# Another order of the attention's extras on four engines

## The chip, the cores and the metric

The kernel runs on one core of one Trainium2 chip. The metric is the device time of one execution in microseconds (us): smaller is better. A core has TensorE (PE, with its weight loads shown as PEld), VectorE (DVE), ScalarE (ACT), GpSimd (POOL) and SyncE (SP, whose queue issues most DMAs). Each takes its own list of instructions in order; they meet in semaphores.

## The reference

One transformer layer with adaptive layer norm, on x of 8 x 512 x 128: an attention with 16 heads of 8 columns, causal, with a layer norm on its output, and then a mixture of 8 experts of which each token uses 2.

```python
mod = (_silu(c) @ wmod).reshape(8, 6, 1, -1)          # sa, ca, ga, sb, cb, gb
h = _layernorm(x) * (1 + ca) + sa
q, k, v = h @ Wq.T, h @ Wk.T * scale, h @ Wv.T
attn = softmax(where(causal, q_heads @ k_heads.T, -inf))
x = x + ga * ((_layernorm(attn @ v_heads) * gamma + beta) @ Wo.T)
h = _layernorm(x) * (1 + cb) + sb
x = x + gb * sum(top-2 experts e: weight_e * (silu(h @ gate_e.T) * (h @ up_e.T)) @ down_e.T)
```

## The kernel before

The attention goes through 8 batches `b` of 512 tokens, each in 4 steps `g` = 0 to 3 of 4 heads; the text calls them the first to the fourth step. Behind its 32 steps comes the loop over 71 tiles of 128 tokens for the experts, which the change doesn't touch.

Each engine has a function `step(b, g)`, a hand-written list of calls for each `g`. TensorE's list is built round two rows of units that take turns. `nat(b, g, k)`, k = 0 to 10 (lines 536 and 538), computes scores of the step two ahead with the tokens on partitions, in bank `psN[k % 4]`, for VectorE's `maxima(k)` (line 1415), which takes each row's maximum. `scores(b, g, u)`, u = 0 to 9 (lines 551 and 553), computes this step's scores transposed, less the maxima, in bank `psT[u % 2]`, for ScalarE's `exps(u)` (line 1098). A `nat` waits for the `maxima` of four units before, a `scores` for the `exps` of two units before. A unit of 512 columns takes 0.22 us on TensorE.

Between these units stand the extras, whose places the change moves:

- `values(b, g, c)`, c = 0 to 3 (line 570): probabilities times v for one chunk of key tokens, 512, 384, 128 and 256 columns wide, each of 4 heads with a weight tile 32 columns wide. They fill bank `psO`; ScalarE's `keep_values` (line 1105) empties it.
- `turn_values` (line 578) transposes that output into `psM`; VectorE's `normalise` (lines 1421, 1425) divides it.
- `turn_max` (line 584) transposes the maxima, split by VectorE into `max_high` and `max_low` (lines 1387, 1392), with a weight tile 32 columns wide; ScalarE's `keep_max` copies them to `mrow` (line 1092), and SP's `max_rows` (line 434) sends them into row 0 and 1 of the next step's stack, for which the next step's `scores` 0 waits.
- `turn_x`, `project_q`, `project_k`, `project_v` (lines 591 to 606): the next batches' x, q, k and v. ScalarE's `x_norm`, `shift_in` and `high`, VectorE's `residue` and `middle` and POOL's `low` split q and k in three bf16 parts; SP sends them out (`q_out`, `k_out`, lines 411, 415) and the stacks for a later step in (`stacks_in`, lines 385, 427, 428).
- `turn_attn` (line 613), `project_o` (line 619) with ScalarE's `o_norm` and `keep_attn` (line 1110) and VectorE's `o_stats`, `mean_var` and `gate_out` (line 1434): the output projection of the batch before.
- `turn_h`, `experts`, `rank` (lines 632 to 656) with ScalarE's `keep_h` (line 1121), `keep_z` and `exp_bids` and VectorE's `route` of 27 short links: the router of the batch two before.

All extras but `values` share the one bank `psM`. `take` on TensorE makes each of them wait until the bank's last user has been read:

```python
def take(free=None):
    if bank[0] is not None:
        pe.wait_ge(*bank[0])
    bank[0] = free
```

SP's queue sets a second order. In the second step (`g == 1`) it first waits for the landing of all six parts of q and k of the next batch, then issues seven DMAs for a stack, and only then `max_rows`:

```python
if g == 1:
    hold("sp", sp, qk_out, 96 * (b + 2))
hold("sp", sp, t_full, UNITS * (4 * b + g))
stacks_in(*step_at(b, g, 3))
max_rows(*step_at(b, g, 1))
```

`k_out` in turn waits for VectorE's `middle` of k (line 1397) and POOL's `low` (line 2035) in the first step. In the last batch's third step VectorE also builds the experts' tile table (`table`, lines 1763 to 1775).

## Time and profile before

| | |
|---|---|
| median of 3 runs | 612.96 us (611.4 to 614.01) |
| the profiled execution | 611.13 us, span 609.4 us |
| TensorE busy | 552.1 us (91%), 5257 matmuls |
| VectorE busy | 470.1 us (77%) |
| ScalarE busy | 404.2 us (66%) |
| GpSimd busy | 244.4 us (40%) |
| chain that ended last | 75% of the span on TensorE, 7% VectorE, 5% issue, 4% DMA |
| granted TensorE clock, mean | 0.966 |

The attention's steps run from about 42 to 358 us of the span, 39.5 to 40.0 us a batch from the third to the sixth; the experts fill the rest. Matmuls overlap in the trace: a row's length is longer than its share of TensorE's time, so the distance from start to start is what a unit costs. A weight load (PEld) with idle time ahead of it doesn't tell by itself whether TensorE waited or was still streaming.

### The profile page before, as it was taken

The page shows a single profiled execution, that of the slowest core. Times are in us where ns is not written, and L with a number is a line of the kernel's source. Part 1 is how long each engine was busy: PE and PEld are TensorE (multiplying, and loading weights), DVE is VectorE, ACT ScalarE, POOL GpSimd, SP SyncE. Part 2 cuts the span into 40 slices and gives each one's busy share as a digit, 9 for nine tenths or more (in the row PEclk, how much of TensorE's full clock was granted, in tenths as well). Part 3 has the DMA queues.
Part 4 walks back from the last instruction along what each step waited for, and adds up shares of the span by engine and source line. Part 5 has one row for each costly group of instructions (what it writes and reads, how often), then busy time and mean ns, then how long its engine had stood idle before and what let it go on. Part 6 is the DMA issues. An engine that isn't in the chain of part 4 may idle for free.

```text
span 609.4 us, 16545 instructions
## 1 busy us (share of the span) xinstructions
PE 552.1 (91%) x5257; PEld 416.9 (68%) x5258; DVE 470.1 (77%) x1593; ACT 404.2 (66%) x715; POOL 244.4 (40%) x328
## 2 busy tenths in 40 slices
PE   5787999999999999999999989999889999999920
PEld 2464555666566566575666549998779999999920
DVE  5899778889899899898998757875846666667635
ACT  4424788888878888788778876765445656565511
POOL 5401301041453643535535345666553333333326
PEclk9597999999999999999999999999999999999975
DMA  4441576732242332333331011122422211111147
GB/s 124 133 139 53 152 209 178 206 98 81 72 123 83 89 105 81 114 88 94 109 98 55 16 42 42 41 58 65 109 67 54 54 44 51 46 46 51 36 176 250
DMA packets 61511, 56.82 MB, mean 93 GB/s; under 512 B 11156, under 2 KB 55572, under 8 KB 61444
## 3 DMA queue, kind: packets, MB, share of 16 engines
q1 hardware_dynamic: 56548, 44.88, 26.6%
q0 software_dynamic: 4320, 8.99, 4.7%
q10 hardware_dynamic: 576, 2.10, 0.9%
q8 instruction: 37, 0.61, 0.4%
q14 instruction: 30, 0.25, 0.1%
HBM read 36.92 MB, written 18.45 MB: 91 GB/s over the span
## 4 chain that ended last, share of the span: by engine, by line
PE 75%; DVE 7%; issue 5%; DMA 4%; ACT 3%; POOL 2%; SPq 1%; another core or an unknown queue 1%; POOLq 0%; ACTq 0%; DVEq 0%
PE psN L970 16%; PE psO L570 13%; PE psO L981 8%; PE psT L551 8%; PE psN L536 7%; PE psT L553 5%; PE psN L538 5%; PE psM L578 2%; DMA probs<-expert_out 2%; DVE negm L1415 1%; PE psM L596 1%; PE psM L601 1%; PE psM L644 1%; PE psM L606 1%; PE psT L957 1%
## 5 line engine op out<-in xcount | busy, mean ns | idle before, releaser
L1415 DVE TENSOR_REDUCE negm<-psN 128x1 f32<-128x512 f32 (+3 forms) x352 | 210.9, 636 | 31.5 <-PE psN L538 27.2
L1098 ACT ACTIVATE probs<-psT 128x512 f32<-128x512 f32 x320 | 180.4, 595 | 40.4 <-PE psT L553 32.1
L970 PE MATMUL psN<-probs 128*128 128x128 f32 x1136 | 139.5, 275 | 0.7 <-issue 0.4
L970 PEld LDWEIGHTS psN<-probs 128*128 128x128 f32 x1136 | 132.6, 192 | 1.6 <-issue 1.5
L2177 POOL DMA_INDIRECT expert_out<-kst_all,dest x71 | 69.1, 973 | 108.2 <-DVE kst_all L1932 98.5
L536 PE MATMUL psN<-kst_all,qst_all 74*128 74x256 bf16 (+2 forms) x384 | 101.2, 281 | 6.2 <-DVE negm L1415 4.1
L551 PE MATMUL psT<-qst_all,kst_all 74*128 74x256 bf16 (+2 forms) x384 | 99.7, 277 | 1.6 <-DMA qst_all<-mrow 0.6
L570 PE MATMUL psO<-probs,vaug 128*32 128x512 f32 (+3 forms) x1024 | 93.7, 444 | 0.1
L538 PE MATMUL psN<-kst_all,qst_all 117*128 117x128 bf16 x512 | 91.7, 222 | 0.0
L1292 ACT ACTIVATE probs<-gu_w 128x1024 f32 x70 | 74.0, 1057 | 24.8 <-PE psN L970 20.0
L1908 DVE TENSOR_TENSOR probs<-probs,psN 128x512 f32<-128x512 f32 x71 | 48.7, 686 | 53.4 <-PE psN L970 22.7
L553 PE MATMUL psT<-qst_all,kst_all 117*128 117x128 bf16 x512 | 85.6, 221 | 0.0
L981 PE MATMUL psO<-down_w,probs 128*128 x568 | 76.4, 278 | 9.3 <-DVE kst_all L1932 8.9
L1300 ACT ACTIVATE probs<-psN 128x512 f32<-128x512 f32 x71 | 42.3, 595 | 61.8 <-PE psN L970 49.5
L981 PEld LDWEIGHTS psO<-down_w,probs 128*128 128x128 f32 x568 | 69.0, 192 | 11.5 <-issue 11.5
L2069 POOL DMA_INDIRECT dispatched<-rows,slots x56 | 56.6, 1010 | 49.4 <-ACT probs L1098 39.9
L536 PEld LDWEIGHTS psN<-kst_all,qst_all 74*128 74x128 bf16 x384 | 38.9, 102 | 41.0 <-DVE negm L1415 22.5
L551 PEld LDWEIGHTS psT<-qst_all,kst_all 74*128 74x128 bf16 x384 | 37.4, 99 | 37.7 <-ACT probs L1098 21.2
L538 PEld LDWEIGHTS psN<-kst_all,qst_all 117*128 117x128 bf16 x512 | 46.8, 100 | 12.9 <-issue 6.3
L553 PEld LDWEIGHTS psT<-qst_all,kst_all 117*128 117x128 bf16 x512 | 50.8, 99 | 1.9
L570 PEld LDWEIGHTS psO<-probs,vaug 128*32 128x32 f32 x1024 | 21.1, 108 | 21.6 <-issue 13.2
L1932 DVE TENSOR_SCALAR kst_all<-psO,dsc 128x128 f32<-128x128 f32 x71 | 24.8, 349 | 13.2 <-PE psO L981 12.6
(242 smaller groups left out, 739.5 us busy)
## 6 DMA issues: line engine op xcount, KB each, us to landing
qst_all<-q_parts_dram SPq DMA_DIRECT2D x96, 96.0 KB
kst_all<-k_parts_dram SPq DMA_DIRECT2D x96, 96.0 KB
kst_all<-dispatched SPq DMA_DIRECT2D x71, 66.0 KB
q_parts_dram<-qparts SPq DMA_DIRECT2D x24, 128.0 KB
k_parts_dram<-kparts SPq DMA_DIRECT2D x24, 128.0 KB
xall<-in_x SPq DMA_DIRECT2D x8, 256.0 KB, 3.4
gu_w<-in_gateT SPq DMA_DIRECT2D x4, 512.0 KB, 5.1
gu_w<-in_upT SPq DMA_DIRECT2D x4, 512.0 KB, 4.9
```

The source lines that it names most:

```text
L536: pe.matmul(psN[:, k % NBANKS, col:col + w - P], qst[g][0:KALL, j, tb * P:(tb + 1) * P], kst[g][0:KALL, j, 0:w - P], start=True, stop=True)
L538: mm = pe.matmul(psN[:, k % NBANKS, col + w - P:col + w], qst[g][0:KMASK, j, tb * P:(tb + 1) * P], kst[g][0:KMASK, j, w - P:w], start=True ...
L551: pe.matmul(psT[:, u % TBANKS, col + P:col + S - P * blk], kst[g][0:KALL, j, blk * P:(blk + 1) * P], qst[g][0:KALL, j, (blk + 1) * P:S], s ...
L553: mm = pe.matmul(psT[:, u % TBANKS, col:col + P], kst[g][0:KMASK, j, blk * P:(blk + 1) * P], qst[g][0:KMASK, j, blk * P:(blk + 1) * P], st ...
L570: mm = pe.matmul(psO[32 * j:32 * j + 32, blk * P:S], vaug[:, blk, g * J + j, :], probs[:, g % 2, o:o + w], start=(c == 0), stop=(c == TB - 1))
L970: mm = pe.matmul(bank[par][:, c * P:(c + 1) * P], ew[par][:, half, c * P:(c + 1) * P], xgT[par], start=True, stop=True)
L981: mm = pe.matmul(psY, hh[par][:, c * P:(c + 1) * P], down_w[:, bass.ds(e, 1), c, :], start=(c == 0), stop=(c == FC - 1))
L1098: nc.scalar.activation(probs[:, g % 2, 512 * u:512 * (u + 1)], psT[:, u % TBANKS, :], ACT.Exp, scale=SOFTMAX_SCALE).then_inc(exp_done, 1)
L1292: nc.scalar.activation(ew[par][:].rearrange("p k f -> p (k f)"), gu_w[:, bass.ds(e, 1)].rearrange("p o k f -> p (o k f)"), ACT.Copy).then_ ...
L1415: nc.vector.tensor_reduce(dst, src, axis=AX.X, op=ALU.max, negate=True).then_inc(nat_done, 1)
L2069: gp.indirect_dma_start(xd[:, :], bass.IndirectOffsetOnAxis(ap=slots_of(b)[:, k, n:n + 1], axis=0), rows_of(b)[:, n, :], None).then_inc(di ...
L2177: gp.indirect_dma_start(yd[:, :], bass.IndirectOffsetOnAxis(ap=dest[u][:, 0:1], axis=0), ysb[u], None).then_inc(y_out[u], 16)
```

## The change

No instruction is added or taken away. In `step` of TensorE, ScalarE and VectorE, calls change places; POOL's and SP's lists stay. TensorE's new lists, with the units as n0 to n10 (`nat`) and s0 to s9 (`scores`) and the `values` as V0 to V3:

```text
step 1 before: n0 s0 n1 s1 V1 n2 s2 turn_values n3 s3 n4 V2 turn_max s4 n5 s5 project_k n6 s6 n7 s7 V3 n8 s8 turn_h n9 s9 n10 experts
step 1 after:  n0 s0 n1 s1 V1 n2 s2 turn_values n3 s3 V2 n4 turn_max s4 n5 s5 project_k n6 s6 V3 n7 s7 n8 turn_h s8 n9 s9 n10 experts
step 2 before: n0 s0 n1 s1 n2 turn_values V0 s2 n3 s3 V1 n4 s4 V2 turn_max n5 s5 n6 V3 s6 n7 s7 project_v n8 s8 n9 s9 V0 V1 n10
step 2 after:  n0 s0 n1 s1 turn_values n2 V0 s2 n3 s3 V1 turn_max n4 s4 n5 V2 s5 V3 n6 s6 n7 s7 project_v n8 s8 V0 n9 s9 V1 n10
step 3 before: n0 s0 rank n1 s1 n2 s2 turn_attn n3 s3 n4 V2 s4 turn_values n5 s5 n6 s6 turn_max n7 s7 n8 V3 s8 n9 s9 project_o n10
step 3 after:  rank n0 s0 n1 s1 n2 V2 s2 turn_attn n3 s3 n4 s4 turn_values n5 s5 n6 s6 turn_max n7 s7 n8 V3 s8 n9 s9 n10 project_o
step 4 before: n0 s0 n1 s1 V0 n2 s2 turn_values n3 s3 n4 s4 V1 n5 s5 n6 s6 n7 turn_max V2 s7 n8 V3 s8 turn_x n9 s9 n10 V0 project_q
step 4 after:  n0 s0 n1 s1 V0 n2 s2 n3 s3 n4 turn_values s4 n5 s5 V1 n6 s6 V2 n7 turn_max s7 n8 V3 s8 n9 s9 turn_x V0 n10 project_q
```

The core of the diff, with the other engines:

```diff
@@ TensorE, first step
-                    if there(b, g, 2):
-                        nat(*step_at(b, g, 2), 4)
                     if there(b, g, -1):
                         values(*step_at(b, g, -1), 2)
+                    if there(b, g, 2):
+                        nat(*step_at(b, g, 2), 4)
                     if there(b, g, 1):
                         turn_max(*step_at(b, g, 1))
...
@@ TensorE, second step
                     scores(b, g, 8)
+                    values(b, g, 0)
                     if there(b, g, 2):
                         nat(*step_at(b, g, 2), 9)
                     scores(b, g, 9)
-                    values(b, g, 0)
+                    values(b, g, 1)
...
@@ ScalarE, first step
                         keep_h(b - 2)
+                    exps(b, g, 8)
                     if there(b, g, -1):
                         keep_values(*step_at(b, g, -1))
-                    exps(b, g, 8)
...
@@ ScalarE, second step: keep_max ahead of exps 4; third o_norm and exp_bids ahead of exps 9
@@ ScalarE, third step: keep_values ahead of exps 9
@@ ScalarE, fourth step: first x_norm ahead of exps 0, fourth ahead of exps 6
@@ VectorE, first step
-                    if there(b, g, 2):
-                        maxima(*step_at(b, g, 2), 0)
                     if there(b, g, 1):
                         max_high(*step_at(b, g, 1))
+                    if there(b, g, 2):
+                        maxima(*step_at(b, g, 2), 0)
...
                         residue(b + 1, k_hi, kparts, kres, k_r1, k_parts)
-                        middle(b + 1, kres, kparts, k_r1, k_mid)
...
                         maxima(*step_at(b, g, 2), 8)
+                    if has_batch(b + 1):
+                        middle(b + 1, kres, kparts, k_r1, k_mid)
+                    if there(b, g, 2):
                         maxima(*step_at(b, g, 2), 9)
...
@@ VectorE, second step: max_high ahead of maxima 0; mean_var behind maxima 4; single route links move by one maximum
@@ VectorE, third step
-                    if has_batch(b - 1):
-                        gate_out(b - 1)
                     if b == B - 1:
                         table(slice(0, N1), nfull, None)
                         V.nop().then_inc(tiles_ready, 1)
+                    if has_batch(b - 1):
+                        gate_out(b - 1)
...
@@ VectorE, third and fourth step: max_high behind maxima 0 and 1; normalise of the fourth behind maxima 4
```

## Rows read from the trace of the kernel before

**Rows 1.** Stretches: width, busy us of each engine (instructions), granted clock, DMA.
```profile
245.50:285.10 39.60, 39.58 (x419) 25.12 (x418) 35.60 (x108) 32.97 (x70) 18.54 (x26) 1.00 0.33 96
...
323.20:357.60 34.40, 33.17 (x346) 19.05 (x343) 27.77 (x97) 28.81 (x59) 14.22 (x20) 1.00 0.14 39
```

**Rows 2.** Waits of the weight loads, 126 to 323 us: total, times, longest.
```profile
PEld psN L536 <- DVE negm L1415: 11.6, 20, 0.8
PEld psT L551 <- ACT probs L1098: 10.3, 24, 0.8
```

**Rows 3.** Timeline around chunks 0 and 1 of values: start, length, [idle before <-releaser].
```profile
257.53 0.10 PEld L551 LDWEIGHTS psT<-qst_all,kst_all 74*128 74x128 bf16 x1 [0.84 <-ACT probs L1098]
...
258.15 0.22 PE L553 MATMUL psT<-qst_all,kst_all 117*128 117x128 bf16 x1
...
259.09 0.28 PE L536 MATMUL psN<-kst_all,qst_all 74*128 74x256 bf16 x1
...
274.81 0.22 PE L553 MATMUL psT<-qst_all,kst_all 117*128 117x128 bf16 x1
...
275.96 0.34 PE L536 MATMUL psN<-kst_all,qst_all 74*128 74x384 bf16 x1
```

**Rows 4.** Timeline, TensorE's weight loads behind three waits.
```profile
253.63 0.29 PEld L641 LDWEIGHTS psM<-confb,onesrow 1*128 1x128 f32 x2 [0.19 <-ACT h2T L1121]
...
267.29 0.10 PEld L551 LDWEIGHTS psT<-qst_all,kst_all 74*128 74x128 bf16 x1 [0.18 <-ACT probs L1098]
...
279.29 0.10 PEld L551 LDWEIGHTS psT<-qst_all,kst_all 74*128 74x128 bf16 x1 [0.21 <-ACT probs L1098]
```

**Rows 5.** Timeline of TensorE, third step: values 2 and turn_max apart.
```profile
268.53 0.22 PE L538 MATMUL psN<-kst_all,qst_all 117*128 117x128 bf16 x1
268.68 0.43 PE L570 MATMUL psO<-probs,vaug 128*32 128x128 f32 x8
269.04 0.28 PE L551 MATMUL psT<-qst_all,kst_all 74*128 74x256 bf16 x1
...
270.40 0.28 PE L553 MATMUL psT<-qst_all,kst_all 117*128 117x128 bf16 x2
...
270.76 0.28 PE L536 MATMUL psN<-kst_all,qst_all 74*128 74x256 bf16 x1
```

**Rows 6.** Timeline of TensorE around values 2 with turn_max, first and fourth step.
```profile
248.31 0.22 PE L538 MATMUL psN<-kst_all,qst_all 117*128 117x128 bf16 x1
...
248.85 0.28 PE L551 MATMUL psT<-qst_all,kst_all 74*128 74x256 bf16 x1
...
279.64 0.22 PE L538 MATMUL psN<-kst_all,qst_all 117*128 117x128 bf16 x1
...
280.17 0.28 PE L551 MATMUL psT<-qst_all,kst_all 74*128 74x256 bf16 x1
```

**Rows 7.** Timeline of TensorE around values 0 and 1, end of second step.
```profile
263.67 0.22 PE L553 MATMUL psT<-qst_all,kst_all 117*128 117x128 bf16 x1
...
265.46 0.40 PE L538 MATMUL psN<-kst_all,qst_all 117*128 117x128 bf16 x4
```

**Rows 8.** Timeline, third step: turn_attn, keep_attn, turn_values.
```profile
267.47 0.42 PEld L613 LDWEIGHTS psM<-identf,onn 128*128 128x128 f32 x4
...
268.22 0.77 ACT L1110 ACTIVATE lnT<-psM,bet,gam 128x512 f32<-128x512 f32 x1
...
269.22 0.42 PEld L578 LDWEIGHTS psM<-identf,oT 128*128 128x128 f32 x4
```

**Rows 9.** Timeline of VectorE, last batch's third step.
```profile
349.98 0.69 DVE L1434 TENSOR_TENSOR proj<-psM,modbc 128x512 f32<-128x512 f32 x1 [0.25 <-PE psM L619]
```

**Rows 10.** SP's queue in the second step; the chain around 232 us.
```profile
256.44 0.76 SPq L385 DMA_DIRECT2D qst_all<-zero_b  x1
...
261.49 1.21 SPq L434 DMA_DIRECT2D qst_all<-mrow  x2
...
231.71 2.93 DMA qst_all<-mrow
```

More of the change, by code:

```diff
@@ L703, in step @@
                     scores(b, g, 6)
+                    if there(b, g, -1):
+                        values(*step_at(b, g, -1), 3)
                     if b == B - 1:
@@ L744, in step @@
                         values(*step_at(b, g, -1), 1)
+                    if there(b, g, 1):
+                        turn_max(*step_at(b, g, 1))
                     if there(b, g, 2):
@@ L788, in step @@
                         nat(*step_at(b, g, 2), 2)
+                    if there(b, g, -1):
+                        values(*step_at(b, g, -1), 2)
                     scores(b, g, 2)
@@ L796, in step @@
                         nat(*step_at(b, g, 2), 4)
-                    if there(b, g, -1):
-                        values(*step_at(b, g, -1), 2)
                     scores(b, g, 4)
@@ L839, in step @@
                     scores(b, g, 2)
-                    if there(b, g, -2):
-                        turn_values(*step_at(b, g, -2))
                     if there(b, g, 2):
@@ L846, in step @@
                         nat(*step_at(b, g, 2), 4)
+                    if there(b, g, -2):
+                        turn_values(*step_at(b, g, -2))
                     scores(b, g, 4)
+                    if there(b, g, 2):
+                        nat(*step_at(b, g, 2), 5)
+                    scores(b, g, 5)
                     if there(b, g, -1):
@@ L850, in step @@
                     if there(b, g, 2):
-                        nat(*step_at(b, g, 2), 5)
-                    scores(b, g, 5)
-                    if there(b, g, 2):
                         nat(*step_at(b, g, 2), 6)
                     scores(b, g, 6)
+                    if there(b, g, -1):
+                        values(*step_at(b, g, -1), 2)
                     if there(b, g, 2):
@@ L859, in step @@
                         turn_max(*step_at(b, g, 1))
-                    if there(b, g, -1):
-                        values(*step_at(b, g, -1), 2)
                     scores(b, g, 7)
@@ L1208, in step @@
                     exps(b, g, 8)
+                    if there(b, g, -1):
+                        keep_values(*step_at(b, g, -1))
                     exps(b, g, 9)
@@ L1211, in step @@
                         keep_spread(LATER[4 * b + g], psM[:])
-                    if there(b, g, -1):
-                        keep_values(*step_at(b, g, -1))
                 elif g == 3:
+                    if has_batch(b + 2):
+                        x_norm(b + 2, (0,))
                     exps(b, g, 0)
@@ L1591, in step @@
                     if has_batch(b - 2):
+                        route(b - 2, 6)
                         route(b - 2, 7)
+                    if there(b, g, 2):
+                        maxima(*step_at(b, g, 2), 3)
                     if has_batch(b - 1):
@@ L1693, in step @@
                     if there(b, g, 2):
-                        maxima(*step_at(b, g, 2), 1)
                         maxima(*step_at(b, g, 2), 2)
-                        maxima(*step_at(b, g, 2), 3)
-                    if there(b, g, -2):
-                        normalise(*step_at(b, g, -2))
                     if there(b, g, 1):
@@ L1701, in step @@
                     if there(b, g, 2):
+                        maxima(*step_at(b, g, 2), 3)
                         maxima(*step_at(b, g, 2), 4)
+                    if there(b, g, -2):
+                        normalise(*step_at(b, g, -2))
                     if has_batch(b - 1):
```

103 lines of the change are left out of this document (47 added, 56 removed).

## The prediction

> **What bounds the kernel now.** I first looked at the stretches of the span [rows 1]. A batch of attention in steady state (the sixth of eight) takes 39.6 us, as do its neighbours; TensorE is busy in practically all of it, at the full granted clock; VectorE is busy 35.6 us of it and ScalarE 33. So in this part the order of TensorE's own queue sets the time, and another engine counts only where TensorE waits for it. In the last batch (323 to 357 us) TensorE has 1.2 us of idle time and ScalarE is the busier neighbour. Behind 357.6 us the experts run; the diff touches nothing there.
>
> Next the list of waits of the weight loads [rows 2]. It claims 11.6 us for VectorE's maxima and 10.3 us for ScalarE's exponentials between 126 and 323 us. Before I believe it I look at where these waits lie. The longest, 0.84 us, follow chunk 0 of `values`, and every other long one a chunk as well: from the last start ahead of it to the first behind it chunk 0 (512 columns) takes 1.15 us, chunk 1 (384) 0.94 [rows 3], the gap growing with the chunk whatever engine is named. That is four heads streaming side by side, hence work. Real waits are what remains where a unit starts later than the same unit does elsewhere. I find three in each batch [rows 4]: the router's `experts` waits 0.19 us for `h2T`; in the fourth step `scores` 6 waits 0.21 us; in the third step `scores` 2 is 0.11 us later than the usual gap of 0.07. Together some 0.45 us a batch, of 39.6. That is all that a better order could win in steady state.
>
> **Groups on TensorE: the main cost.** Two kinds of work use a weight tile 32 columns wide: `values` (128x32) and `turn_max` (128x32). All others load 128 columns. I compare starts of matmuls on either side, and take off the 0.06 us at which 128-column matmuls follow each other. A start inside a row with x2 is its start plus its length less one matmul's 0.22.
> - `values` 2 alone: 268.53 to 269.04, so 0.51 - 0.06 = 0.45. `turn_max` alone: 270.46 to 270.76, so 0.24. Together 0.69 [rows 5].
> - The two side by side, in the first step: 248.31 to 248.85, 0.48; in the fourth, in the other order: 279.64 to 280.17, 0.47 [rows 6].
> - `values` 0 alone: 274.81 to 275.96, 1.09; `values` 1 alone: 258.15 to 259.09, 0.88; together 1.97 [rows 3]. Side by side at the end of the second step: 263.67 to 265.46, 1.73 [rows 7].
>
> So a group of 32-column work costs about 0.24 us for going in and coming out, whatever its length. The diff parts such pairs three times in a batch: `nat` 4 comes between `values` 2 and `turn_max` in the first step (+0.21), `nat` 9 and `scores` 9 between `values` 0 and 1 in the second (+0.24), `nat` 7 between `values` 2 and `turn_max` in the fourth (+0.22). In the second step `turn_max` goes from `values` 2 to `values` 1: as many groups, nothing. `turn_values` and `values` 0, side by side before, are parted too, but `turn_values` is 128 wide and its group was separate already: nothing. Each of the three pairs exists 7 times (the first batch lacks the one in step one and has a `spread` inside the one in step two; the last batch has no `turn_max` in step four): 7 x 0.67 = **+4.7 us**.
>
> The rows show what happens at such a border: `values` 2 starts 0.15 us behind the last matmul's start, where a 128-column start comes 0.06 behind the one before [rows 5]. A rule against this reading, which the sum doesn't use: the Trainium skill ("TensorE: Matmul & The Clock Gate", Step-by-step: what each phase is for) says that TensorE pulls a weight load ahead of matmuls in flight, by which a border would be hidden and the three parted pairs would be free; the trace differs, the border costs 0.24 us. The skill's page "TensorEngine Tiling (Array Packing)", Key Properties, says "Mode switching requires drain", without a price; with it the pairs cost what the rows show.
>
> **Waits that go.** (a) In the first step `turn_h` now stands before `scores` 8 and `keep_h` before the output's `keep_values`, so one unit more lies between `turn_h` and `experts`: the 0.19 us goes, in 6 batches, 1.1 us. What is late next is `k_r1`, VectorE's residue of k, which the new, earlier `turn_h` needs for its bank and which I find due 0.05 us ahead of it: nothing, 0.1 a batch at most. (b) Fourth step: `values` 1 moves behind `scores` 5, so its 0.8 us lies between `scores` 4 and 6 and covers the exponential that `scores` 6 waits for: 0.15 us net in 6 batches, 0.9. (c) Third step: `rank` moves ahead of `nat` 0, `values` 2 ahead of `scores` 2, which then is late enough: 0.08 in 5 batches, 0.4. Sum **-2.4 us**.
>
> **A wait that comes.** In the third step `values` 2 lay between `turn_attn` and `turn_values`. Both use bank psM: `turn_values` may start once ScalarE's `keep_attn` has emptied it. Now `turn_attn` loads at 267.47, `keep_attn` runs from 268.22 to 268.99, `turn_values` starts at 269.22 [rows 8], 1.75 us after `turn_attn`. Without `values` 2 (0.45) it would come after 1.30, but the bank takes 268.99 - 267.47 = 1.52 and 0.05 for the semaphore: 0.27 to 0.29 us of wait, with `nat` 5 and all later units behind it. `scores` 5 would have waited 0.16 for its exponential anyway and is covered by it. 6 batches: **+1.7 us**.
>
> **Moved at no cost,** each with its cover. The maxima's high parts: the low part is done over 2 us before `turn_max` in the third step and nearly 1 us before it in the fourth, where `turn_max` also moves back; a unit (0.6 us) later is hidden, and costs what it is late if it isn't. In that step `normalise` comes after `maxima` 4, but still ahead of the later `turn_max`. The second step's routing links change places with maxima of the same length. `turn_x` is a unit later and directly ahead of `values` 0, whose 1.1 us and `nat` 10 cover `shift_in` on ScalarE; without this cover `project_q` would wait its whole 0.8 us. ScalarE: `keep_values` and `x_norm` fill idle time in front of `exps` 0 of step four. `gate_out` waits 0.2 us longer for the later `project_o`, and `nat` 2 of the fourth step, which waits for the maxima behind it, has more than that in hand (0.2 if not). POOL only sees later inputs: o_inv by 0.5 us, low part of k by 1.4 (below).
>
> **The last batch.** ScalarE binds here, so the parted pair in its second step (0.24, counted above) is probably swallowed, and in the third step `turn_values`, with `values` 2 no longer ahead of it, starts 0.2 earlier. In its third step the tile table comes before `gate_out`. VectorE no longer waits 0.25 us for `project_o` [rows 9], but `turn_values` of the fourth step, which takes the bank that `gate_out` frees, waits for 3.2 us of table, up to 1.5 us. The experts' start doesn't hang on that: it hangs on POOL's shift of the second layer norm, behind VectorE's stretch of clears and statistics, which the table merely precedes as before. Together (-0.24, -0.2, -0.25) **-0.7 us**, between -0.7 and +1.5 if the experts follow TensorE after all.
>
> **Sum.** 4.7 - 2.4 + 1.7 - 0.7 = +3.3 us. The profiled execution took 611.13 us (span 609.4), which is 1.8 below the median of the runs, 612.96; so 614.4 for a like execution and **616.3 us** by the median.
>
> **Rivals.**
> - *The borders are hidden.* If a load can be pulled ahead once the neighbours change, or the time lost at a border is taken back from a wait behind it, 4.7 falls to nothing, leaving -2.4 + 1.7 - 0.7: 611.6 us, not slower. It decides at +1.4 us for the three pairs together, 0.07 a border. For it: waits exist behind borders (0.45 a batch). Against: equal borders cost equal time at each place [rows 3, 5, 6, 7]. Chance 0.15, with 611 to 613.5.
> - *SP's queue becomes late in step three.* `middle` of k moves behind `maxima` 8: 0.47 + 0.60 us of maxima and a wait for `nat` 8, 1.2 to 1.4 us. POOL's low part and k's DMAs follow, SP holds the next stacks for their landing (256.44), and the maxima's rows are queued behind these (261.49) [rows 10]. Rows then are issued at 262.9 and 263.5; with the median 1.7 us that the DMA view gives they land at 265.2, with a long one, 2.93 us [rows 10], at 266.4. `scores` 0 of step three starts at 265.86 + 0.45 for parted pairs + 0.4 for `rank`, 266.7. So a slack of 1.5 us, or 0.3 at worst; it decides from a landing of 3.2 us. The stacks themselves, whose landing no row gives here, have some 3 us from their last issue to `nat` 0. Failing everywhere it costs up to 1.4 us x 6, so 618 to 624. Chance 0.15.
> - *The listed waits are real.* Then 22 us in five batches [rows 2], 35 in eight, can shrink with the order; a tenth of that is 3.5 us: 609.5. Against it stands that the gap grows with the chunk. Chance 0.08.
> - The forecast's own case, 614.5 to 618: 0.55. Unnamed, mostly longer: 0.07.
>
> **How the numbers follow.** A measurement of this kernel can tell about 0.5% from no change, 3.1 us: faster is below 609.9, slower above 616.0. Forecast's case: 0.31 above, 0.24 below that. Slower 0.31 + 0.15 + 0.07 = 0.53; same 0.24 + 0.13 = 0.37; faster 0.08 + 0.02 = 0.10. The range leaves out the third rival and the upper half of the second: 611 to 621.
>
> **What would show it.** In the profile after: batches of 40.0 to 40.2 us in place of 39.6; `turn_max` alone in steps one and four, with 0.24 around it; no wait of `experts` for `h2T`; a wait of `turn_values` for `lnT` of 0.2 to 0.3 us in each third step; `scores` 6 of the fourth step without one. I am wrong if the three parted pairs don't lengthen their stretches by 0.2 us each, or if waits for `mrow` or `k_parts_dram` come up in the third step.

## The result, and the profile after

The changed kernel takes 620.6 us (median of 6 runs, 619.08 to 625.91) where the kernel before took 612.74 beside it (6 runs, 610.09 to 614.01): the medians lie 7.9 us apart. The ratio, which goes by all twelve runs and not by the two medians, is 1.015, interval 1.0126 to 1.0175, or 9.2 us. The profiled execution took 619.87 us, its span is 618.1. A second group of runs on another occasion gave 1.0147 (1.0114 to 1.018). The direction and the range of the prediction held; the size was 8 to 9 us, not 3.3.

First the stretches of the kernel after, to be held against [rows 1]: the first batch, the third, the sixth, and two short pieces (columns as there).

```profile
41.20:89.30 48.10, 42.22 (x364) 22.92 (x363) 35.94 (x107) 30.38 (x58) 7.31 (x6) 0.89 0.43 115
129.07:169.36 40.29, 40.22 (x419) 25.16 (x418) 35.74 (x109) 33.19 (x71) 13.68 (x21) 1.00 0.29 85
250.14:291.22 41.08, 40.55 (x419) 25.18 (x418) 36.12 (x109) 33.46 (x71) 18.50 (x26) 1.00 0.32 93
...
78.40:82.00 3.60, 3.60 (x20) 1.35 (x20) 1.59 (x5) 1.72 (x5) 0.00 (x0) 0.56 0.86 206
409.20:412.60 3.40, 3.40 (x19) 3.40 (x18) 2.13 (x18) 2.61 (x3) 1.03 (x2) 0.50 0.08 26
```

The third batch is what was forecast, 40.29 us with TensorE busy in all of it. Two others are not: the sixth has 0.5 us in which TensorE is idle, and the first takes 48.1 us, 3.3 more than in the trace of before. In two pieces TensorE counts as busy throughout, but the granted clock is near 0.5, that is 1.2 GHz: one at the start of the first batch's fourth step, one in the experts' part.

Next, the timeline of TensorE in the third batch: `values` 2 and `turn_max` in the first step, now with `nat` 4 between them, and `turn_values` in the third step. These rows answer to [rows 6] and [rows 8].

```profile
132.56 0.22 PE L553 MATMUL psT<-qst_all,kst_all 117*128 117x128 bf16 x1
132.71 0.42 PE L570 MATMUL psO<-probs,vaug 128*32 128x128 f32 x8
133.06 0.28 PE L536 MATMUL psN<-kst_all,qst_all 74*128 74x256 bf16 x1
133.18 0.22 PE L538 MATMUL psN<-kst_all,qst_all 117*128 117x128 bf16 x1
133.34 0.23 PE L584 MATMUL psM<-identb,mparts 128*32 128x128 bf16 x1
133.50 0.28 PE L551 MATMUL psT<-qst_all,kst_all 74*128 74x256 bf16 x1
...
154.23 0.42 PEld L578 LDWEIGHTS psM<-identf,oT 128*128 128x128 f32 x4 [0.24 <-ACT lnT L1110]
```

From 132.56 to 133.06 is 0.50 us for `values` 2, from 133.18 to 133.50 is 0.32 for `turn_max`; less 0.06 each, 0.70, where the pair side by side took 0.48 [rows 6]. And `turn_values` waits 0.24 us for `keep_attn`, as the prediction said (0.27 to 0.29).

What it did not say is in the list of waits. Of the weight loads' waits between 60 and 345 us, those that name a DMA, first in the kernel after and then the two places where they are longest:

```profile
PEld psN L536 <- DMA kst_all<-k_parts_dram: 2.0, 2, 1.4
PEld psT L551 <- DMA qst_all<-mrow: 1.3, 4, 0.4
```
```profile
77.16 0.10 PEld L536 LDWEIGHTS psN<-kst_all,qst_all 74*128 74x128 bf16 x1 [1.44 <-DMA kst_all<-k_parts_dram]
...
272.58 0.10 PEld L536 LDWEIGHTS psN<-kst_all,qst_all 74*128 74x128 bf16 x1 [0.55 <-DMA kst_all<-k_parts_dram]
...
272.99 0.10 PEld L551 LDWEIGHTS psT<-qst_all,kst_all 74*128 74x128 bf16 x1 [0.30 <-DMA qst_all<-mrow]
```

The kernel before has no wait for `k_parts_dram` in this stretch. The first of these, `nat` 0 of the first batch's fourth step, lasts 1.44 us, and the half clock from 78.1 to 81.5 us follows it, some 1.7 us more (an estimate: half of the 3.4 us). The second stands at the head of the sixth batch's third step. The second is what the prediction had named as the sign that it is wrong, a wait for `mrow` or `k_parts_dram` in a third step; the first, in a fourth step, it had not thought of. Both point at SP's queue.

### The profile page after: what moved, and what is told of

The parts are those of the page before. It is cut to its first block, busy times and chain, and to the rows that moved or that the text cites. A ratio compares the mean times of both kernels' runs of the same rounds, so it can differ in the third digit from the quotient of the medians.

```text
span 618.1 us, 16545 instructions
## 1 busy us (share of the span) xinstructions
PE 560.4 (91%) x5257; PEld 418.1 (68%) x5258; DVE 471.4 (76%) x1593; ACT 407.2 (66%) x715; POOL 244.3 (40%) x328
## 4 chain that ended last, share of the span: by engine, by line
PE 69%; DVE 9%; issue 6%; DMA 5%; ACT 4%; SPq 3%; POOL 2%; another core or an unknown queue 1%; ACTq 0%; POOLq 0%; DVEq 0%
PE psN L970 15%; PE psO L570 12%; PE psO L981 8%; PE psN L536 7%; PE psT L551 6%; PE psN L538 4%; PE psT L553 4%; PE psM L578 2%; DVE negm L1414 2%; DMA probs<-expert_out 2%; DMA kst_all<-k_parts_dram 1%; PE psM L596 1%; PE psM L601 1%; SPq L427 1%; PE psM L644 1%
## 5 line engine op out<-in xcount | busy, mean ns | idle before, releaser
L1414 DVE TENSOR_REDUCE negm<-psN 128x1 f32<-128x512 f32 (+3 forms) x352 | 213.3, 634 | 35.3 <-PE psN L538 33.5
L570 PE MATMUL psO<-probs,vaug 128*32 128x512 f32 (+3 forms) x1024 | 95.9, 448 | 0.1
L570 PEld LDWEIGHTS psO<-probs,vaug 128*32 128x32 f32 x1024 | 20.3, 108 | 19.7 <-issue 10.8
```

Of the source, the lines that this page charges most:

```text
L570: mm = pe.matmul(psO[32 * j:32 * j + 32, blk * P:S], vaug[:, blk, g * J + j, :], probs[:, g % 2, o:o + w], start=(c == 0), stop=(c == TB - 1))
L1414: nc.vector.tensor_reduce(dst, src, axis=AX.X, op=ALU.max, negate=True).then_inc(nat_done, 1)
```

## The experiments

Two theories. *Pairs*: the three parted pairs carry the loss, 4.7 us, and the rest is scatter. *Queue*: besides the pairs the later `middle` of k makes its DMAs late, and with them stacks and maxima's rows. The runs came in four groups, each beside the kernel before, whose median was 610.72, 611.07, 600.05 and 600.58 us: in the last two groups the experts' part is 8 to 10 us shorter in the traces of the same kernel. So ratios are compared, and a ratio is turned into us with its own group's median.

Step lengths, below, are from `nat` 0 or `rank` of one step to that of the next, in the third to fifth batch where nothing else is said. For the kernel before they are 10.10, 10.87, 8.24 and 10.38 us, for the changed one 10.26, 11.11, 8.43 and 10.49 (the fifth batch's fourth step is up to 0.7 us longer and left out).

**The pairs side by side again, in the changed kernel.**

```diff
@@ TensorE, first step (second and fourth alike)
-                    if there(b, g, -1):
-                        values(*step_at(b, g, -1), 2)
                     if there(b, g, 2):
                         nat(*step_at(b, g, 2), 4)
+                    if there(b, g, -1):
+                        values(*step_at(b, g, -1), 2)
                     if there(b, g, 1):
                         turn_max(*step_at(b, g, 1))
```

> The changed kernel with only the three parted pairs side by side again (values 2 with turn_max in the first and the fourth step, values 0 with values 1 in the second). Theory G (a group of 32-column work costs 0.24 us): 21 groups fewer, -4.7 us against the changed kernel, so about +3.5 to +4.5 us against the kernel before, and the whole batches 40.3 -> 39.6 us. Theory S (the time was lost in waits for DMAs and in the clock that fell behind them, and the borders are hidden): within 1 us of the changed kernel, +7 to +8 us, batches still 40.2 us or more.

Measured: 615.44 us, ratio 1.0093 (1.0065 to 1.0121), 5.7 us over before. First, second and fourth steps are back at 10.03 to 10.22, 10.87 and 10.25, but third steps are 8.5 to 8.7, with nine waits for the maxima's rows, 2.9 us together, and three for `k_parts_dram`, 1.6 us. So the pairs are not all: more than half of the loss stays without them.

**The pairs parted, in the kernel before.** The reverse edit, nothing else.

> The kernel before with only the three pairs parted, all other orders as before. Theory G: +4.7 us against the kernel before, batches 39.65 -> 40.3 us. Theory S: 0 to +1 us, the batches as before. If both hold in part, the batches tell: +0.21, +0.24 and +0.22 us in steps one, two and four.

Measured: 615.24 us, ratio 1.0075 (1.0055 to 1.0095): 4.6 us. First, second and fourth steps 10.33, 11.11 and 10.58, that is 0.23, 0.24 and 0.20 longer; no wait for `k_parts_dram` between 60 and 345 us. The pairs' term is settled, in size and in place. A batch of it (166.89 to 207.13 us) beside one of the unaltered kernel traced in the fourth group (163.13 to 202.52 us); first the latter:

```profile
163.13:202.52 39.39, 39.39 (x419) 25.25 (x418) 35.67 (x108) 33.00 (x70) 18.48 (x27) 1.00 0.33 97
```
```profile
166.89:207.13 40.24, 40.24 (x419) 25.13 (x418) 35.79 (x108) 33.27 (x70) 18.50 (x26) 1.00 0.33 95
```

TensorE counts as busy for 0.85 us more with the same 419 instructions: the border is inside its busy time. Of the 0.85, some 0.15 is not the borders': in this trace `scores` 6 of the fourth step starts as late as in the first trace of the kernel before, and in the one shown it doesn't (more on this below).

**k's middle early again, in the changed kernel.**

```diff
@@ VectorE, first step
                         residue(b + 1, k_hi, kparts, kres, k_r1, k_parts)
+                        middle(b + 1, kres, kparts, k_r1, k_mid)
...
                         maxima(*step_at(b, g, 2), 8)
-                    if has_batch(b + 1):
-                        middle(b + 1, kres, kparts, k_r1, k_mid)
-                    if there(b, g, 2):
```

> The changed kernel with k's middle part directly behind its residue again, as before. If SP's queue comes late because of it (theory Q), the stacks of the third step are issued 1.2 to 1.4 us earlier, the single wait of nat 0 for k_parts_dram in the sixth batch's third step (0.8 us in the changed kernel's profile) goes, and the time falls by 1 to 2 us. If such waits are chance of the DMAs' landing (rival), they come at other places as often and the time stays within 1 us of the changed kernel. The first batch's stack is issued in the third step, not behind k's middle: its wait should stay either way.

Measured: 618.71 us, ratio 1.014 (1.0117 to 1.0164). The trace says more than the time: every wait for `k_parts_dram` behind 60 us is gone, that of the first batch too, which I had expected to stay; third steps are 8.43 in the third to seventh batch, and the last batch begins 3 us earlier than in the changed kernel (327.5 against 330.6 us). But the profiled execution has two pieces of half clock in the experts' part, from 406.8 and 430.7 us, 3.4 us each, where the changed kernel had one, and its span is only 1.6 us shorter. Whether they go with the kernel was open, so it was run again in the last group:

> The changed kernel with k's `middle` directly behind `residue`, once more and with more rounds (the first time its ratio was 1.014, with half-clock pieces of 1.7 us each near 407 and 431 us in the profile, though attention had become 3 us shorter). If the experts' half-clock pieces only happened to fall into it, the ratio is 1.008 to 1.010: 4.5 us for the parted pairs and 0.5 for the rest. If they go with the kernel, again 1.014, a lower mean clock than before's, and a half-clock piece between 360 and 440 us in the profile.

Measured: 606.04 us, ratio 1.0088 (1.0065 to 1.0111): 5.3 us. The profile again has one such piece, from 404.5 us, but so has the kernel before in that group (below). The two intervals of the same kernel do not overlap: the ratio from four runs was off by more than its interval says. The half clock goes with it: the mean granted clock of those four runs is 0.961, of the kernel before beside them 0.964; in the repeat it is 0.964 and 0.963. By the repeat, what the middle costs inside the change is 1.0147 - 1.0088, 0.6% or 3.5 us; by the first group, 1.015 - 1.014, it would be 0.6 us.

**The experts' weights loaded in other steps, in the changed kernel.** Their 12 DMAs on SP are issued in steps 9 to 14 instead of 1 to 6 (`if isinstance(b, int) and 9 <= G * b + g <= 14`).

> The changed kernel with the loads of the experts' weights (12 of 512 KB) issued in steps 9 to 14 instead of 1 to 6. Theory W (in the first batch the stacks land late because they share the DMA engines with these loads; TensorE waits, its clock falls to 0.5 for 3.4 us, which costs another 1.7): the third and fourth step of the first batch shrink from 9.3 and 12.1 us to about 7.9 and 10.4, -3 us in all, unless the later batches now wait instead. Rival (the order of the calls itself makes these two steps long): they stay at 9.3 and 12.1 us.

Measured: 618.06 us, ratio 1.0124 (1.0101 to 1.0146). The first batch heals (third step 7.86, fourth 10.44), but third steps of the third to sixth batch are now 9.22, 8.67, 8.43 and 9.11, and the fourth step of the fourth batch 11.59. So the first batch's wait needs both, k's late parts and the traffic of the weights (the DMA share is 0.86 in the piece from 78.4 us above). In the third and fourth batch, where the weights are now loaded, waits have come up; the sixth batch's was there before.

**k's middle late, alone, in the kernel before.** The reverse of the middle's edit.

> The kernel before with one part of the change alone: k's `middle` behind maxima 8 instead of directly behind `residue`. Theory D (the later `middle` delays k's DMAs; SP holds the next stacks for their landing, and the waits for `k_parts_dram` in the first and sixth batch, 2.7 us together in the profile of the changed kernel, come from it alone, with the clock's fall to 0.56 behind the first): about +2.7 us over before, of it 2 to 3 in steps three and four of the first batch, in which nat 0 of step four waits for k_parts_dram for 0.5 us or more and a piece of half clock follows; steady batches as before, 39.6. Rival E (these waits need the 0.8 us later second half of the steps as well, from the parted pairs and `rank`): no wait for k_parts_dram, at most 0.2 us more.

Measured: 616.5 us, ratio 1.0102 (1.0074 to 1.013): 6.2 us from one line. That line runs 0.95 us later: in the sixth batch it starts 7.30 us behind the first step's start in the kernel before (second trace, step at 242.09) and 8.35 here (step at 248.41; 8.25 in the other batches). The two rows, in this order:

```profile
249.39 0.43 DVE L1397 CAST kparts<-kres 128x512 bf16<-128x512 f32 x1
```
```profile
256.76 0.41 DVE L1397 CAST kparts<-kres 128x512 bf16<-128x512 f32 x1
```

The waits that name a DMA, 60 to 345 us:

```profile
PEld psT L551 <- DMA qst_all<-mrow: 4.2, 10, 0.9
PEld psN L536 <- DMA kst_all<-k_parts_dram: 2.3, 3, 1.3
```

The first batch shows the long wait and the half clock (77.3 to 80.7 us), as theory D had it. But it goes on in steady state, which I had not expected: third steps are 8.61 to 9.01 us instead of 8.24, since `scores` 0 waits for the maxima's rows, which SP issues behind the stacks.

**Pairs and middle together, in the kernel before.**

> The kernel before with two parts of the change: the three pairs parted (4.5 us alone) and k's `middle` behind maxima 8 (6 us alone, by ratio). If the two add, 10.5 us more than before, ratio 1.017. Theory O (they overlap: the parted pairs lengthen TensorE's way to the third step by 0.45 us, and by so much a row of maxima or a stack may come later before anything waits; the changed kernel, which has both and `rank` earlier on top, is only 9 us over before): third steps 8.2 to 8.4 us instead of the 8.6 of the middle alone, first batch still with a wait for k_parts_dram; 7 to 9 us more, ratio 1.012 to 1.015.

Measured: 610.55 us, ratio 1.0162 (1.0136 to 1.0187): 9.7 us, where 4.6 and 6.2 add to 10.8. These two parts alone make as large a loss as the whole change (1.0147 to 1.015). The overlap is small but visible: third steps of 8.20 in the fourth and fifth batch, 8.51 in the third, where the late middle alone had 8.6 to 9.0. The first batch repeats itself, half clock included:

```profile
78.30:81.70 3.40, 3.40 (x18) 1.36 (x17) 1.36 (x3) 1.97 (x5) 0.00 (x0) 0.50 0.84 209
```

**The changed kernel without these two, all else kept.**

> The changed kernel with the three pairs side by side and k's `middle` early, and nothing else undone. Theory (pairs and middle are the whole loss): ratio 1.001 to 1.003, third steps 8.43, the last step 8.6 with no effect on the end. Rival (the three small places, `turn_values` of the third step, the last batch's first step and the table first, matter by themselves, since with all five undone the ratio was 1.0007): 1.004 to 1.006.

Measured: 601.14 us, ratio 1.0007 (0.9992 to 1.0021). No wait for `k_parts_dram`; the last step is 7.34 us, without a cost at the end. In the trace the batches are 39.57 against 39.39 for the unaltered kernel (the third step 8.43 against 8.20, the first 10.03 against 10.10), some 1.0 us over six batches, which the times cannot tell from nothing.

**Three small places as before, in the changed kernel.**

```diff
@@ TensorE, third step
-                    if there(b, g, -1):
-                        values(*step_at(b, g, -1), 2)
                     scores(b, g, 2)
...
                         nat(*step_at(b, g, 2), 4)
+                    if there(b, g, -1):
+                        values(*step_at(b, g, -1), 2)
                     scores(b, g, 4)
@@ TensorE, first step of the last batch: values 3 and scores 8 between count_head and turn_h
@@ VectorE, last batch: gate_out ahead of the table
```

> The changed kernel with three places as before: `values` 2 of the third step between nat 4 and scores 4 again; `gate_out` of the last batch ahead of the table again; `values` 3 and scores 8 of the last batch's first step between `count_head` and `turn_h` again. Theory: each place pays by itself. Third steps 0.2 us shorter in six batches (8.43 to 8.2), `turn_values` no later than in before; the last batch's first step 9.97 to 9.5; the last step 8.69 to 7.0, of which the start of the experts shows no more than 0.3, since it hangs on VectorE's statistics and POOL. Together 1.2 + 0.5 + 0.3, 2 us less than the changed kernel, ratio to before about 1.011 where the changed kernel had 1.015. Rival (the last step's length is paid in the experts' start): 3.3 us less, ratio 1.009. Second rival (the third step's time only moves to scores 5 and to what waits behind it): 0.8 us less.

Measured: 619.78 us, ratio 1.0145 (1.0099 to 1.0191), no gain that this interval could show. The places themselves answered: the last batch's first step is 9.53 instead of 9.97, the last step 6.76 instead of 8.69, with the experts from their fourth tile on no earlier for it (46.6 us behind the last batch's start, 46.3 in the changed kernel). The third step went back by only 0.09 us, to 8.34, not by 0.2: now `scores` 2, which `values` 2 no longer covers and from which `rank` has gone away too, waits for its exponential (0.46 us from `nat` 2 to it, 0.22 in the unaltered kernel).

**All five undone, in the changed kernel.**

> The changed kernel with all the causes named so far undone: the three pairs side by side, k's `middle` directly behind `residue`, `values` 2 of the third step behind nat 4, `gate_out` ahead of the table, and `values` 3 between scores 7 and nat 9 in the last batch's first step. What is left of the change are the later `turn_values` and `turn_x`, `rank` ahead of nat 0, the maxima's high parts and the moved routing links. Theory (the account closes): batches 39.5 to 39.7, no wait for k_parts_dram, no half-clock piece before 580 us, profile 609 to 611.5, ratio 0.998 to 1.002. Rival (something unnamed is left, as the third step's 8.34 us against 8.24 hints): batches 39.8 or more, ratio 1.004 or more.

Measured: 600.68 us, ratio 1.0007 (0.9994 to 1.0019), the same as with two undone. The account closes: the three small places are worth nothing that can be measured.

**Table first, alone, in the kernel before.**

> The kernel before with `gate_out` of the last batch behind the tile table, alone. Theory (the prediction's term for the last batch): the last step becomes 1.5 to 2 us longer on TensorE (`turn_values` waits for the bank that gate_out frees), the experts start no later, and the end is the same within 0.5 us; ratio 1.000. Rival (the changed order of work at the start of the experts goes with the piece of half clock near 407 us, which three of the four kernels with the table first showed there and none with gate_out first): a piece of half clock between 360 and 412 us, 1.7 us more, ratio 1.003. Second rival (TensorE's last step sets the experts' start): 1.5 us more without any such piece.

Measured: 599.51 us, ratio 0.9986 (0.9968 to 1.0004). The last step is 7.82 us instead of 6.51, the end no later, and there is no piece of half clock between 54 and 572 us. Both rivals fall: in the last batch TensorE does not set the experts' start, and the half clock near 407 us does not come with this order each time.

**The two moves that were booked as gains, in the kernel before.**

```diff
@@ TensorE, first step; on ScalarE keep_values behind exps 8
-                    scores(b, g, 8)
                     if has_batch(b - 2):
                         turn_h(b - 2)
+                    scores(b, g, 8)
@@ TensorE, fourth step
-                    if there(b, g, -1):
-                        values(*step_at(b, g, -1), 1)
                     if there(b, g, 2):
                         nat(*step_at(b, g, 2), 5)
                     scores(b, g, 5)
+                    if there(b, g, -1):
+                        values(*step_at(b, g, -1), 1)
```

> The kernel before with two moves of the change alone, those that the prediction booked as gains: `turn_h` ahead of scores 8 (with `keep_values` behind exps 8 on ScalarE) and `values` 1 of the fourth step behind scores 5. Theory (the prediction's terms (a) and (b)): no wait of `experts` for h2T, first steps 0.14 to 0.19 us shorter in six batches; scores 6 of step four without a wait, 0.15 us in six; together 1.7 to 2.0 us less than before, ratio 0.997. Rival (what one wait gives back the next takes, because VectorE or ScalarE is what is short): batches within 0.1 us of before, ratio 1.000.

Measured: 613.96 us, ratio 1.0031 (1.0007 to 1.0056): 1.9 us slower, not 1.7 to 2.0 faster. The first step gains 0.07 us (10.03), and the wait of `experts` for `h2T` is gone as forecast; the fourth step loses 0.4 (10.74 to 10.76, where it was 10.38 in the first trace of before and 10.23 in the second). TensorE's weight loads in it:

```profile
159.83 0.10 PEld L536 LDWEIGHTS psN<-kst_all,qst_all 74*128 74x128 bf16 x1
159.88 0.10 PEld L538 LDWEIGHTS psN<-kst_all,qst_all 117*128 117x128 bf16 x1
160.57 0.10 PEld L551 LDWEIGHTS psT<-qst_all,kst_all 74*128 74x128 bf16 x1 [0.59 <-ACT probs L1098]
160.59 0.21 PEld L553 LDWEIGHTS psT<-qst_all,kst_all 117*128 117x128 bf16 x2
160.90 0.16 PEld L570 LDWEIGHTS psO<-probs,vaug 128*32 128x32 f32 x8
```

With `values` 1 behind it, `scores` 5 is the third unit in a row without an extra between, and waits 0.59 us for its exponential: an `exps` takes 0.60 us, a `nat` with its `scores` 0.45 or less.

**`values` 3 beside the pairs on top of that.** In the first, second and fourth step `values` 3 follows `values` 2 or `turn_max` directly, so that three groups of 32-column work fewer remain in a batch.

> The kernel of the run with two moves, and `values` 3 put beside `values` 2 and `turn_max` in the first, second and fourth step, so that each batch has three groups of 32-column work fewer than before. Theory G (a group costs 0.24 us wherever it stands): 3 x 0.24 x 7 = 5.0 us less than the two-moves kernel, steady batches 0.7 us shorter, ratio to before 0.989. Rival (now VectorE, at 35.6 of 39.6 us, and ScalarE bind between the groups, since 0.9 us of 32-column work in one piece leaves the units behind it without cover): less than half of that, with new waits of scores for the maxima behind the long group, ratio 0.994 or above.

Measured: 615.4 us, ratio 1.007 (1.0048 to 1.0093): 4.3 us slower. Third to fifth batches are 40.1 us. The cover went with the borders: first steps 10.40 instead of 10.03, and of the fourth step only 0.2 us is won. The price of a border, 0.24 us, is paid anew by parting, but this gathering did not save it: an extra between two units also hides what VectorE and ScalarE still owe.

**The whole fourth step of the change, with its pair kept, in the kernel before.** All four engines' fourth step as changed, `turn_max` and `values` 2 side by side, and `turn_h` ahead of `scores` 8.

> The kernel before with the whole fourth step of the change (all engines: x's transposes and the values' transposes later, `values` 1 behind scores 5, the maxima's high and low part later), but with `turn_max` and `values` 2 side by side, and with `turn_h` ahead of scores 8 in the first step. Theory (what is worth something in the change is `turn_values` directly ahead of scores 4, which gives VectorE and ScalarE the time that `values` 1 behind scores 5 took from them in the two-moves run): fourth steps 10.25 us in steady state instead of 10.38, first steps 10.04, batches 39.4 to 39.5 instead of 39.6; 1.0 to 1.5 us less than before, ratio 0.998, profile 608 to 610. Rival (the fourth step of the changed kernel was short only because its batches as a whole ran later against the DMAs' landings): fourth steps 10.4 and more, ratio 1.000 to 1.005.

Measured: 600.12 us, ratio 1.0005 (0.9989 to 1.0021). Fourth steps 10.20, first steps 10.03, batches 39.30, the shortest seen; but the unaltered kernel has 39.39 in that surrounding, and the difference is below what the times show. So `turn_values` ahead of `scores` 4 does give `scores` 5 the cover that it lacked in the run with two moves; it gains nothing over the order of before.

**Both kernels unaltered, once more.**

> The changed kernel once more, unaltered, beside the others of this group on the same chip, so that the experiments' ratios can be set against its own. By theory, 1.010 to 1.017 of before. Whether its three irregular pieces repeat is open: the wait for k_parts_dram in the first batch should (the queue makes it late each time); the 0.8 us in the sixth batch and the half clock near 409 us need not, if they depend on when a DMA happens to land.

Measured: 608.1 us, ratio 1.0147 (1.0114 to 1.018). In the first batch `nat` 0 again waits for `k_parts_dram`, 0.58 us this time, without half clock behind it; the first batch is 45.68 us. The sixth batch's third step is 8.54 and its wait for `k_parts_dram` is gone, one of 0.3 us stands in the second batch; there are eight waits for the maxima's rows, 2.8 us together, where the first trace had four, 1.3 us.

> The kernel before, unaltered, for a trace on this chip. In the first trace scores 6 of the fourth step waited 0.15 us for its exponential and the step took 10.38 us; in the run with the table first, which leaves that step alone, it took 10.23. If the wait was a matter of that execution, it is absent here and the step takes 10.23; if it belongs to the kernel, 10.38. Ratio 1.000.

Measured: 601.1 us, ratio 1.0007 (0.9986 to 1.0028). The fourth step takes 10.23 us and `scores` 6 waits for nothing; nor does `scores` 2 of the third step, whose length is 8.20. So two of the three waits in [rows 4] are not there every time. They differ: the one of `scores` 2 stands in the first trace alone, but `scores` 6 is 0.11 to 0.14 us later in all three traces of the first two groups that keep the old order there (the kernel before, the pairs parted, the middle late) and in none of the last two (table first, two parts, this one). It goes with the occasion, and why is not known.

## Why the prediction came out so, point by point

**Groups on TensorE, +4.7: right.** 4.6 us alone, in the places and sizes named. The steps that a pair was parted in are 0.20 to 0.24 us longer. Of the two rules that the prediction weighed, this agrees with the Trainium skill's "TensorEngine Tiling (Array Packing)", Key Properties, by which changing the tiling mode drains TensorE; that a drain is what takes the time, no run shows. By the Trainium skill's "TensorE: Matmul & The Clock Gate", Step-by-step: what each phase is for, a weight load is pulled ahead of matmuls in flight where the row groups do not conflict or it goes to the background weight buffer, and the parting could be free; across a change from 128 to 32 columns no run shows that.

**Waits that go, -2.4: mis-sized, some -0.4.** (a) The wait of `experts` went, but 0.07 us a batch is left of its 0.19, since the moved `scores` 8 now follows `turn_h`. (b) and (c), 0.9 and 0.4 us, were read from one execution and are absent in the next trace of the same kernel; (b)'s wait was there in the first two groups only. The reason given for (b), that `values` 1 covers the exponential of `scores` 6, leaves out what it uncovered: `scores` 5. Alone the move costs 0.4 us a batch; only `turn_values` ahead of it in the changed kernel brings that to nothing.

**A wait that comes, +1.7: right in kind, 1.4 in size.** 0.24 us of wait in the third step, whose length went from 8.20 to 8.43: 1.4 us in six batches. The way back is not open, though: with `values` 2 back in its place, `scores` 2 waits.

**The last batch, -0.7: within its bounds, with one wait overlooked.** Table first costs nothing at the end, as said (0.8 us less alone, interval -1.9 to +0.2), though `turn_values` waits 1.19 us for `gate_out`. But in the last batch's first step `turn_h` waits for the count's bank, since `values` 3 and `scores` 8 no longer lie between `count_head` and it:

```profile
337.89 0.42 PEld L632 LDWEIGHTS psM<-identf,rows 128*128 128x128 f32 x4 [0.44 <-DVE counts L1559]
```

That the experts' start hides this too is shown only together with the other two small places.

**Moved at no cost, and the rival of SP's queue: this is the step that failed.** The prediction saw the chain (`middle`, POOL's low part, k's DMAs, SP's hold, the stacks, the maxima's rows), put it at 1.2 to 1.4 us later, gave it a slack of 1.5 us or 0.3 at worst, and a chance of 0.15. Here is SP's queue in the sixth batch, first of the unaltered kernel (second trace, third step at 263.05 us), then of the changed one (third step at 271.51 us); they answer to [rows 10].

```profile
251.16 1.32 SPq L415 DMA_DIRECT2D k_parts_dram<-kparts  x3
253.86 0.76 SPq L385 DMA_DIRECT2D qst_all<-zero_b  x1
...
258.92 1.21 SPq L434 DMA_DIRECT2D qst_all<-mrow  x2
```
```profile
260.81 1.31 SPq L415 DMA_DIRECT2D k_parts_dram<-kparts  x3
265.49 0.76 SPq L385 DMA_DIRECT2D qst_all<-zero_b  x1
...
270.54 1.21 SPq L434 DMA_DIRECT2D qst_all<-mrow  x2
```

From the end of k's last issue to the first DMA behind the hold it is 253.86 - 252.48 = 1.38 us in the one, 265.49 - 262.12 = 3.37 in the other. From the maxima's rows to the third step it is 4.1 us in the one and 1.0 in the other, with 1.7 needed to land.

The delay of k's first issue was sized about rightly: counted from the first step's start it is 1.6 us here and 1.1 to 1.2 in the changed kernel's second trace, of it 0.2 because `residue` itself starts later behind the parted pair; the prediction had 1.2 to 1.4. **What failed is the slack.** It was counted with k's landing as fast as in the kernel before, while only the rows' landing was let vary. And k's landing didn't stay: whatever SP's hold takes goes straight through its queue to stacks and rows. In the third to seventh batch of all seven traces with the late `middle` the hold takes 1.7 to 3.6 us, and it is no scatter: 2.8 to 3.2 in the third batch and 2.8 to 3.6 in the sixth, each time. In the eleven traces with the early `middle` the third batch has 1.39 or 1.40 us, the sixth 1.38 to 1.42 with one exception of 3.19, and only the fifth is regularly long, 1.9 to 2.5. So the line cost two delays, 0.9 to 1.6 us until k's DMAs are issued and up to 2 us of a longer landing.

In the first batch it is not the hold, which takes 1.4 us in every trace. There, with the experts' weights in the same queue, the stack issued at 71.69 us is there for `nat` 0 only at 77.1; the kernel before issues it at 71.58, 0.1 us earlier on the clock and 0.7 earlier behind the batch's start, and `nat` 0 doesn't wait at 76.33. First the changed kernel, then the kernel before:

```profile
71.69 0.53 SPq L428 DMA_DIRECT2D kst_all<-k_parts_dram  x1
72.71 1.21 SPq L434 DMA_DIRECT2D qst_all<-mrow  x2
73.96 1.09 SPq L455 DMA_DIRECT2D gu_w<-in_gateT  x2
```
```profile
71.58 0.53 SPq L428 DMA_DIRECT2D kst_all<-k_parts_dram  x1
```

The prediction had given these stacks some 3 us and no landing time at all.

The rival's price, 1.4 us in each of six batches, was too high in steady state (third steps 0.4 to 0.8 us longer in the third to fifth batch with the late `middle` alone) and left out the first batch, which lost 3 us in the changed kernel's first trace against the one with the middle early again (48.06 and 45.08).

**The sum with measured terms:** 4.6 for the pairs, 3.5 for the middle inside the change, 1.4 for `turn_values`, -0.4 for the waits: 9.1 us, where the two groups gave 9.2 (0.015 of 612.74) and 8.8 (0.0147 of 600.05). That this fits so well is partly luck, since the middle's 3.5 comes from the repeat alone; the two parts are not independent either. With the middle undone first, it is worth 3.5 us and the pairs then 4.9 (1.0088 - 1.0007); with the pairs undone first, they are worth 3.2 (1.0147 - 1.0093) and the middle 5.2 (1.0093 - 1.0007). The terms of `turn_values` and of the waits, 1.0 together, rest on the traces alone: with pairs and middle undone the ratio is 1.0007, 0.4 us, which is within its interval.

**Left open.** Why k's landing takes up to 2 us longer behind the late `middle`, and in the third and sixth batch most of all, was not tried and is not known. Nor is it explained why the piece of half clock near 400 us comes in some executions.

## What to carry to other kernels

Count the slack of a queue with a slow landing of every DMA that the queue is held for, not only of the last one, and don't take a landing time from the old schedule over into the new one; a line that ran 0.95 us later on VectorE cost more here (6.2 us) than three added borders a batch on TensorE (4.6). An extra between two units has two prices, its own border and the cover that it gives: moving it changes both, and a gain read from one wait needs the question which unit is uncovered. A wait of 0.1 to 0.2 us seen in one profiled execution is no term of a sum until a second trace, best taken on another occasion, shows it as well.

## What the runs showed of the hardware

With much the same work and idle time TensorE gets a piece of half clock in one execution and none in another. The kernel before in the second trace: 393.5 to 397.6 us, then to 401.0, and after it.

```profile
393.50:397.60 4.10, 3.54 (x31) 3.30 (x29) 2.92 (x12) 2.08 (x3) 3.25 (x8) 1.00 0.20 54
397.60:401.00 3.40, 3.40 (x17) 3.40 (x17) 1.19 (x9) 2.54 (x3) 1.14 (x2) 0.50 0.18 56
401.00:405.00 4.00, 4.00 (x38) 4.00 (x37) 3.12 (x21) 2.25 (x3) 2.30 (x3) 1.00 0.21 56
```

About the same place of the work (within 1 us, counted from the last batch's start) in the changed kernel, second trace:

```profile
402.00:406.00 4.00, 3.44 (x31) 3.20 (x29) 3.59 (x16) 2.52 (x4) 3.15 (x8) 1.00 0.21 53
406.00:410.00 4.00, 4.00 (x36) 4.00 (x36) 1.85 (x16) 2.44 (x3) 2.08 (x3) 1.00 0.17 50
```

In both TensorE is idle for 0.56 us in the row ahead. The one is then at 0.50 of the full clock for 3.4 us, with 17 groups where 36 were done in 4 us, which costs some 1.7 us (an estimate, half of 3.4); the other stays at 1.00. Such pieces go with the scatter between runs of one kernel: of the changed kernel's six runs in the third group the slowest, 612.71 us, had a mean granted clock of 0.955, the two quickest, 606.45 and 606.79, had 0.967. A long wait can be paid twice in this way: of the six traces in which `nat` 0 of the first batch's fourth step waits for `k_parts_dram`, the four with waits of 1.27, 1.28, 1.44 and 1.49 us show a piece of half clock right behind it, the two with 0.88 and 0.58 do not.
